# Splitting the three closing sums of a mixture-of-experts decoder layer between VectorE and GpSimd

## The reference, cut to what matters

```python
x = x + attn(layernorm(x)); x = x + xattn(layernorm(x))
# the last block
shared = silu_mul(h @ shared_gate_up.T) @ shared_down.T * sigmoid(h @ shared_gate_vec.T)
for e in range(16):                       # top 4 of 16 experts per token
    sparse += silu_mul(h @ gate_up[e].T) @ down[e].T * combine[:, e]
x = x + shared + sparse
```

## Time and profile before

| | us |
|---|---|
| three timed executions, median | 995.27 |
| lowest and highest of them | 993.92 and 996.04 |
| the profiled execution | 985.83 |
| its span, first to last instruction | 983.8 |
| TensorE busy in the span | 949.0 |
| VectorE busy | 723.6 |
| GpSimd busy | 408.5 |

### The profile page before, as it was taken

One profiled execution on the slowest core, in us unless ns is written; L12 is line 12 of the kernel. 1 busy time (PEld: TensorE's weight loads), 2 busy tenths in 40 slices (PEclk: granted clock), 3 DMA queues, 4 the chain that ended last, 5 costly groups with the idle time before them and its releaser, 6 DMA issues.

```text
span 983.8 us, 18292 instructions
## 1 busy us (share of the span) xinstructions
PE 949.0 (96%) x6081; PEld 836.6 (85%) x6081; DVE 723.6 (74%) x1523; ACT 379.0 (39%) x1063; POOL 408.5 (42%) x320
## 2 busy tenths in 40 slices
PE   7999999999999999999999999888999999999996
PEld 6788888988898888888898888777888799999985
DVE  6878967877877889667888777646777666666647
ACT  3546443442234643233544333431352344444420
POOL 1312313163521245563225365306706366666660
PEclk9999999999999999999999999989999999999999
DMA  7863397321079922236877501350142477777768
GB/s 268 306 238 138 118 354 288 147 87 65 1 246 368 356 87 72 80 103 219 298 261 244 198 35 45 135 233 26 67 172 78 95 121 121 119 118 120 119 113 297
DMA packets 64841, 161.17 MB, mean 164 GB/s; under 512 B 6640, under 2 KB 40304, under 8 KB 63600
## 3 DMA queue, kind: packets, MB, share of 16 engines
q1 hardware_dynamic: 50304, 140.97, 40.6%
q0 software_dynamic: 14448, 19.05, 11.9%
HBM read 84.72 MB, written 75.27 MB: 163 GB/s over the span
## 4 chain that ended last, share of the span: by engine, by line
PE 86%; issue 4%; DVE 4%; POOL 2%; ACT 2%; DMA 1%; SPq 0%; DVEq 0%; ACTq 0%
PE bank L487 12%; PE bank L489 11%; PE bank L488 11%; PE bank L717 11%; PE bank L735 6%; PE bank L567 6%; PE bank L863 4%; PE bank L865 3%; PE bank L553 3%; PE bank L590 3%; PE bank L592 3%; PE bank L591 2%; POOL xs L1208 2%; PE bank L834 2%; PE bank L824 2%
## 5 line engine op out<-in xcount | busy, mean ns | idle before, releaser
L1200 POOL TENSOR_TENSOR rot<-turn 128x512 f32<-128x512 f32 x64 | 94.2, 1472 | 283.6 <-DVE rtotal L1357 216.2
L1368 DVE SCALAR_TENSOR_TENSOR turn<-bank,bqk,trig 128x1024 f32<-128x1024 f32 x128 | 162.2, 1279 | 29.0 <-PE bank L489 26.0
L1263 POOL DMA_INDIRECT sums<-ysb,token_at x79 | 123.1, 1558 | 69.5 <-DVE ysb L1736 35.2
L1230 POOL TENSOR_TENSOR kv<-c_t,v_t 128x512 f32<-128x512 f32 x64 | 67.8, 1071 | 134.6 <-PE bank L592 69.0
L717 PE MATMUL bank<-wo,z_t 128*128 128x256 f32 x512 | 116.0, 379 | 0.8 <-ACT z_t L1066 0.8
L487 PE MATMUL bank<-xt_hi,w_hi 128*128 128x512 f32 x256 | 105.3, 411 | 1.7 <-DVE xt_lo L1332 1.7
L717 PEld LDWEIGHTS bank<-wo,z_t 128*128 128x128 f32 x512 | 94.9, 190 | 12.8 <-ACT z_t L1066 1.0
L1058 ACT COPY prob_t<-bank 128x512 f32<-128x512 f32 x64 | 37.5, 586 | 163.3 <-PE bank L553 163.3
L489 PE MATMUL bank<-xt_hi,w_lo 128*128 128x512 f32 x256 | 100.1, 391 | 0.0
L1024 ACT ACTIVATE prob<-prob,negmax 128x128 f32<-128x128 f32 x256 | 99.0, 390 | 2.5 <-DVE negmax L1353 2.4
L488 PE MATMUL bank<-xt_lo,w_hi 128*128 128x512 f32 x256 | 99.7, 390 | 0.0
(11 more groups left out here) (181 smaller groups left out, 2285.7 us busy)
## 6 DMA issues: line engine op xcount, KB each, us to landing
xs<-zeros SPq DMA_DIRECT2D x16, 2120.0 KB, 13.6
w_hi<-w_dram SPq DMA_DIRECT2D x24, 768.0 KB, 4.3
w_lo<-w_dram SPq DMA_DIRECT2D x24, 768.0 KB, 7.2
xe_all<-xs SPq DMA_DIRECT2D x79, 132.5 KB, 2.6
sums<-zeros SPq DMA_DIRECT2D x3, 2176.0 KB, 18.3
raw<-in_wqkv SPq DMA_DIRECT2D x16, 384.0 KB, 4.2
w_dram<-w_hi SPq DMA_DIRECT2D x8, 768.0 KB, 6.6
w_dram<-w_lo SPq DMA_DIRECT2D x8, 768.0 KB, 8.5
```

What stands on the lines that cost most here:

```text
L1200: nc.gpsimd.tensor_tensor(rot[m][1][:], turn[m][1], turn[m][2], ALU.add).then_inc(rot_pool, 1)
L1263: nc.gpsimd.indirect_dma_start(sums_dram[s % SUMS], bass.IndirectOffsetOnAxis(ap=token_at[:, s:s + 1], axis=0), ysb[s % YBUFS][:], None, c ...
L1368: last = nc.vector.scalar_tensor_tensor(turn_all[m][:, 2 * i:2 * i + 2, :], qk_bank[2 * m + i][:].unsqueeze(1).to_broadcast([128, 2, GT]), ...
```

## The change

GpSimd adds the three sums of groups 1 and 2 (batches 4 to 11), six additions of 128x1024, after its last scatter. VectorE adds those of groups 3 and 0, two pieces after chunks 1, 3 and 4. SP loads the pieces of each sum in the order 3, 0, 1, 2 and stores groups 1 and 2 after the new semaphore `pool_comb_done`.

```diff
+SUM_ORDER = (3, 0, 1, 2)
...
             for i in LAST_SUMS:
                 sp.wait_ge(y_stored[i], 16 * len(range(i, SLOTS, SUMS)))
-                for j in range(GROUPS):
+                for j in SUM_ORDER:
                     rows = sums_dram[i][j * GT:(j + 1) * GT, :]
                     sp.dma_start(ys[j][:, i], rows.rearrange("(b p) d -> p b d", b=GB)).then_inc(ys_loaded[i][j], 16)
-            for j in range(GROUPS):
-                sp.wait_ge(comb_done, GROUPS * (SUMS - 1) + j + 1)
-                for half in range(2):
-                    b = GB * j + 2 * half
-                    if j == GROUPS - 1:
-                        sp.wait_ge(acc_added, b + 2)
-                    sp.dma_start(out[:, b:b + 2, :], x[:, b:b + 2, :]).then_inc(stored, 16)
+            def store(b):
+                sp.dma_start(out[:, b:b + 2, :], x[:, b:b + 2, :]).then_inc(stored, 16)
+
+            sp.wait_ge(comb_done, 2 * SUMS)
+            store(0)
+            store(2)
+            for j in (1, 2):
+                sp.wait_ge(pool_comb_done, 2 * (SUMS - 1) + j)
+                store(GB * j)
+                store(GB * j + 2)
+            for b in (BATCH - GB, BATCH - 2):
+                sp.wait_ge(acc_added, b + 2)
+                store(b)
...
+            for i in range(SUMS):
+                pool.wait_ge(y_stored[i], 16 * len(range(i, SLOTS, SUMS)))
+            for nth in range(SUMS):
+                for j in (1, 2):
+                    xj = x[:, GB * j:GB * (j + 1), :]
+                    pool.wait_ge(ys_loaded[LAST_SUMS[nth]][j], 16)
+                    if j == 1 and nth == 0:
+                        pool.wait_ge(acc_added, GB * (GROUPS - 1))
+                    if nth:
+                        pool.wait_ge(pool_comb_done, 2 * (nth - 1) + j)
+                    nc.gpsimd.tensor_tensor(xj, xj, ys[j][:, LAST_SUMS[nth]], ALU.add).then_inc(pool_comb_done, 1)
...
-                    dve.wait_ge(comb_done, GROUPS * nth)
+                    dve.wait_ge(comb_done, 2 * nth)
                 nc.vector.tensor_tensor(xj, xj, ys[j][:, LAST_SUMS[nth]], ALU.add).then_inc(comb_done, 1)
 
             dve.wait_ge(acc_added, GB * (GROUPS - 1))
             for i in range(SCH):
                 shared_mult(GROUPS - 1, i)
-                if 1 <= i <= 4:
-                    for j in range(2):
-                        combine((i - 1) // 2, 2 * ((i - 1) % 2) + j)
-            for j in range(GROUPS):
-                combine(SUMS - 1, j)
-            dve.wait_ge(comb_done, SUMS * GROUPS)
+                if i in (1, 3, 4):
+                    for j in (3, 0):
+                        combine((1, 3, 4).index(i), j)
+            dve.wait_ge(comb_done, 2 * SUMS)
             shared_add(GROUPS - 1)
```

More of the change, by code:

```diff
@@ L334, in decoder @@
         comb_done = sem("comb_done")
+        pool_comb_done = sem("pool_comb_done")
         stored = sem("stored")
```

## The result

Seven executions of the changed kernel took 999.08 us in the median (996.72 to 1001.35), seven of the kernel before 994.25 (992.32 to 996.04). The ratio is 1.0048, 95% interval 1.0031 to 1.0065, which lies clear of 1: the changed kernel is slower. The forecast was 2.4 us, or 1.0024.

The account below looks back on a forecast made before the run. VectorE's queue of additions after chunk 5 was taken to set the end. Chunk 5 later +5.1, additions gone -4.7, down product +1.25, clock +0.7 gave +2.4 us on 995.27: 997.7 us, range 994.8 to 999.8.

Parts of the forecast that it names:

- The turns: VectorE and GpSimd additions with both inputs in SBUF exclude each other, one instruction each; chunk 5 5.1 us late; chance 0.82.
- start of chunk 5: VectorE's multiplication of chunk 5 after the contended additions, forecast at 978.8 instead of 973.67, 5.1 us late.
- The wait for the last scatter: GpSimd's first addition also waits for the last scatter into sum 0, so starts at about 963.1, not 961.8.
- TensorE's clock: Chunk 5's down product may run at the lower clock after TensorE idles; costs 0 to 1.25 us, 0.7 taken.
- the sum: At the end: chunk 5 +5.1, four additions -4.7, down product +1.25, clock +0.7; +2.35, rounded to +2.4 us.
- The last store: Issued by SP after shared_add, forecast at 983.3 instead of 980.92.
- every shift of the issue of the last store shifts the end by as much: At the kernel's end: landing 2.4 us after the last store's issue and 0.5 us more to the end stay unchanged.
- The rival without exclusion: VectorE's and GpSimd's additions overlap freely; last store issued 1.0 us earlier, 994.3 us; chance 0.08.
- GpSimd keeps its turn: GpSimd's back-to-back additions are not interrupted, VectorE gets only gaps; last store +5.0 us, 1000.3 us; chance 0.06.
- The removal of the four additions: VectorE's four additions behind chunk 5 go, 4.70 us; TensorE's 1.25 us down product remains; alone brings 3.4 us.

Follow-up runs that it names:

- e5: Changed kernel with VectorE's six additions taking their second input from a PSUM bank instead of the loaded piece; ratio to the kernel before 1.0003, tail 29.5 us.
- e7: Changed kernel without VectorE's six additions, GpSimd's kept; one execution, no ratio, tail 29.6 us.
- e9: Changed kernel with GpSimd waiting for each sum's last scatter only ahead of that sum's two additions; ratio to the kernel before 1.0020, tail 31.2 us.
- e2: Changed kernel measured again with no edit, twelve executions; ratio to the kernel before 1.0030, tail 32.0 us.
- e8: Changed kernel without GpSimd's six additions, VectorE's kept; one execution, no ratio, tail 26.9 us.
- e12: Kernel before, plus a GpSimd wait until shared_add is finished and a small memset nothing reads; ratio to the kernel before 1.0024, tail 31.7 us.
- e3: Changed kernel with chunk 5 multiplied on VectorE ahead of its last two additions; ratio to the kernel before 1.0042, tail 33.2 us.

## Why the prediction was right, and where it was short

**The turns** came out as worked out, from a row 870 us earlier and with operations of other sizes. Forecast for VectorE after 966: four additions of 1.8 to 3.6 us; measured 2.63, 3.39, 2.79 and 3.36. Forecast for GpSimd: 2.36 twice, then 3.0 to 3.4; measured 2.39 and 2.36, then 3.32 to 3.36. Forecast start of chunk 5: 978.8 - 955.0 = 23.8 us after the last scatter; measured 23.7. e5 and e7 show the cause.

**The wait for the last scatter** was placed at 8.1 and came at 7.96. e9 shows what it costs: chunk 5 2.7 us later, but at the end only 0.4.

**TensorE's clock.** I took 0.7 us between 0 and 1.25; it was 2.08 - 1.25 = 0.83, at the lower level. VectorE's wait between chunk 5 and `shared_add` was 2.25 us where the sum had 1.95.

**The last store** was forecast at 28.3 after the last scatter and was issued at 28.5.

**What was missing** is the step from the last store to the end. I took it as unchanged: 2.4 us to land and 0.5 us more. In the changed kernel the last store landed 2.0 us after its issue, at 30.5, and the span ended at 31.6, because GpSimd's last addition ended at 25.87 and the program ended 5.7 us after that. The term "every shift of the issue of the last store shifts the end by as much" failed there: about 0.6 us that the sum didn't have, of which 0.4 came back by the quicker landing; with the rest of the sum 0.2 to 0.3 short, the tail is 2.85 us longer instead of 2.4. The profile before gave no sign of it, since GpSimd's last instruction was done 27 us before the end and its closing DRAIN 16 us before it.

**The size.** Tail 2.85 us longer in the first pair of traces and 3.5 in e2 against the mean of before; measured 4.8 (3.1 to 6.5) and 3.0 us (1.8 to 4.2). The forecast of 2.4 lies below the first interval and inside the second. Of the distance to 4.8, 0.5 us is in the tail, the missing term above all; the rest is scatter between executions, as far as these runs tell. The direction and the turns came out for the reason given. That 999.08 us lies inside the range, which ended at 999.8, was in part luck: 4.8 us is twice the forecast, and the traces account for only 2.85 of it.

**The rival without exclusion** was mispriced. I gave it 994.3 us, 1.0 faster. e5 is that kernel, and it measured 1.0003 with a tail 1.0 us longer than the mean of before. So even with no exclusion the split gains nothing: GpSimd ends at 23.8 and the program 5.7 us later. Without that the gain would still have been small: the last store landed at 27.9, and with the 0.4 us of before from there to the end the tail would be 28.3, an estimate, 0.2 less than before. (In its working GpSimd ends (2,2) at 972.8, 968.1 + 2 x 2.36, and not at 972.5; nothing hangs on it.) **GpSimd keeps its turn** didn't occur in any trace: VectorE got in between GpSimd's instructions each time.

**The removal of the four additions** was priced at 3.4 us if nothing took their place. e8 gave 1.6: 0.7 went because chunk 5 was 0.7 late there, 0.4 in GpSimd's closing DRAIN, and the rest because eight stores in a row take longer to land.

## What to carry to other kernels

Before splitting elementwise work over VectorE and GpSimd, look for a place in the trace where both work at once with all inputs in SBUF: if one's duration jumps to the other's end, the two are one engine for such work, as they were here, and the split adds GpSimd's slower time to the sum. Give GpSimd the part whose partner on VectorE reads PSUM, and let GpSimd's program, its waits included, be over well before the last store: here the end came 5.7 us after GpSimd. And compare tails, or stages, and not spans, when the position of an unchanged stage moves by 10 us between executions.

## What the runs showed of the hardware that was not expected

- The program ends 5.7 us after the end of GpSimd's last instruction or later, whether that is an addition of 2.3 to 3.3 us (five traces) or a memset of 0.10 us (e12). With no such instruction but a late wait it ended 5.7 us after the DRAIN behind the wait started (e8); 5.45 us of that is the DRAIN.
- Durations of VectorE hold the time in which it is locked out (3.39 us for 1.23 us of work); no view of idle time or waits shows it.
- An operation moved by 1.95 us on VectorE ended 2.3 us later on account of one more GpSimd instruction ahead of it (e3).
- The start of the same last scatter lay between 955.0 and 968.2 us in fourteen traces of kernels that are equal up to it.
